# Loading first expert weights during attention, and one stage for output projection and row scaling

## The reference

```
x = x + attn_a(layernorm(x))             # 16 heads of 16, causal
    out = softmax(q k^T / 4) v           # per head
    attn_a = out @ Wo.T
n = layernorm(x);  x = x + n + moe(rmsnorm(n) * norm_scale)
    logits = t @ gate_w + gate_b; top 2 of 8 experts, softmax weights
    expert: swiglu(t @ w1 + b1) @ w2 + b2        # w1: 256 x 1024, w2: 512 x 256, each of 8 experts
x = x + attn_b(layernorm(x));  x = x + ffn(layernorm(x))
```

## Time and profile before

| | |
|---|---|
| median of 3 runs | 1952.26 us |
| the profiled execution, its own time | 1949.15 us |
| its span | 1947.3 us |
| PE busy | 1743.7 us (90%) |
| DVE busy | 1333.4 us (68%) |
| ACT busy | 826.5 us (42%) |
| POOL busy | 786.7 us (40%) |
| mean granted clock of PE | 0.93 of full speed |
| data moved by DMA | 152.83 MB, mean 78 GB/s |

### The profile page before, as it was taken

One profiled execution on the slowest core, in us unless ns is written; L12 is line 12 of the kernel. 1 busy time (PEld: TensorE's weight loads), 2 busy tenths in 40 slices (PEclk: granted clock), 3 DMA queues, 4 the chain that ended last, 5 costly groups with the idle time before them and its releaser, 6 DMA issues. The chain is left out here.

```text
span 1947.3 us, 32655 instructions
## 1 busy us (share of the span) xinstructions
PE 1743.7 (90%) x8300; PEld 977.3 (50%) x8301; DVE 1333.4 (68%) x2681; ACT 826.5 (42%) x1660; POOL 786.7 (40%) x771
## 2 busy tenths in 40 slices
PE   6979999999998667599999999699975899999997
PEld 3533443434443457356666666344444566666664
DVE  5648888878784258677776777437878577776764
ACT  3424666656666212333333333246664233333332
POOL 4341111111111004256666666243542566666663
PEclk9988999999999896599999999799995899999998
DMA  4653342424330584432222222300123222222322
GB/s 135 167 133 74 94 100 72 100 67 100 80 84 23 171 244 166 165 63 43 46 46 43 49 43 43 90 27 1 44 87 133 59 47 43 45 46 43 49 43 30
DMA packets 116124, 152.83 MB, mean 78 GB/s; under 512 B 17552, under 2 KB 98192, under 8 KB 112976
## 3 DMA queue, kind: packets, MB, share of 16 engines
q1 hardware_dynamic: 79632, 106.28, 19.7%
q0 software_dynamic: 31808, 37.32, 12.0%
q10 hardware_dynamic: 4608, 8.39, 1.2%
HBM read 86.47 MB, written 56.69 MB: 74 GB/s over the span
## 5 line engine op out<-in xcount | busy, mean ns | idle before, releaser
L502 DVE TENSOR_REDUCE a_mx<-a_p_sn 128x1 f32<-128x512 f32 (+3 forms) x640 | 371.8, 631 | 91.5 <-PE a_p_sn L541 62.9
L475 ACT ACTIVATE a_Pt<-a_p_st 128x512 f32<-128x512 f32 (+2 forms) x624 | 306.9, 577 | 194.2 <-PE a_p_st L555 179.1
L1232 ACT ACTIVATE e_y<-e_yb,wt 128x256 f32<-128x256 f32 x142 | 72.1, 508 | 502.9 <-DVE e_yb L1259 502.9
L1192 PE MATMUL e_p_y<-w,e_hT 128*128 x1136 | 271.2, 382 | 2.0 <-ACT e_hT L1226 2.0
L1171 PE MATMUL e_p_g<-w,e_tT 128*128 x568 | 270.6, 599 | 0.0
L1171 PE MATMUL e_p_l<-w,e_tT 128*128 x568 | 268.0, 594 | 0.0
L1192 PEld LDWEIGHTS e_p_y<-w,e_hT 128*128 128x128 f32 x1136 | 216.9, 191 | 92.3 <-issue 66.4
L538 PE MATMUL a_p_sn<-Kst,Qst 96*128 96x512 bf16 (+3 forms) x768 | 248.9, 344 | 8.0 <-DMA Qst<-qk_parts 5.5
L451 POOL TENSOR_SCALAR_AFFINE_SELECT a_Pt<-a_Pt 128x512 f32<-128x512 f32 x128 | 81.5, 637 | 422.3 <-ACT a_Pt L475 422.3
L555 PE MATMUL a_p_st<-Qst,Kst 99*128 99x512 bf16 (+3 forms) x768 | 215.9, 334 | 15.6 <-ACT a_Pt L475 13.1
L1080 POOL DMA_INDIRECT xs<-t_rows,token x142 | 140.3, 988 | 99.9 <-DVE token L1018 48.3
(11 more groups left out here) (208 smaller groups left out, 2532.7 us busy)
## 6 DMA issues: line engine op xcount, KB each, us to landing
qk_parts<-a_part SPq DMA_DIRECT2D x64, 192.0 KB, 2.8
a_Vst<-V SPq DMA_DIRECT2D x16, 512.0 KB, 16.3
o_rows<-a_OT ACTq DMA_DIRECT2D x32, 256.0 KB, 2.1
a_Ot<-o_rows SPq DMA_DIRECT2D x32, 256.0 KB, 3.5
...
```

What stands on the lines that cost most here:

```text
L475: act.activation(weights(kb, slice(h, h + n), a, b), p_st[:, i % RING, 0:n * (b - a)].rearrange("p (n w) -> p n w", n=n), ACT.Exp, scale=D ...
L502: dve.tensor_reduce(mx[:, hs[0]:hs[-1] + 1, place], p_sn[:, (s + k) % RING, 0:w * len(hs)].rearrange("p (h w) -> p h w", w=w), AX.X, ALU.m ...
L1192: mm = pe.matmul(p_y[:, s, 0:D], hT[:, s, k * P:(k + 1) * P], g["w2"][:, bass.ds(e, 1), k, :].rearrange("p a n -> p (a n)"), start=(k == 0 ...
```

## The change

`V` and `w1` now share one tensor `VW`: it holds 16 blocks of 4 KB per partition, which are the values of unit u during attention and one half of an expert's `w1` after it. In each SP step of `attend_a`, `load_w1(u)` writes the half u over the values of unit u, which `load_v(u)` has read by then. `project_out` and `scale_rows` become one phase `out_rows`, written out for 41 steps without a loop. In step j, tile j is turned and divided, tile j-1 turned back, tile j-2 multiplied and added with its statistics, the square roots and coefficients are made for groups of four tiles (steps 4c+5 and 4c+6), tile j-6 is normalised by ACT (it was DVE), j-7 scaled and turned, j-8 copied and made into logits. `Ot` is loaded for two tiles at a time, three slots deep, by five DMAs: four of 16 rows (the dimensions of one head, 1 KB runs) and one of the four rows of sums, so 68 rows rather than 128. The second square root is now of var(1+eps)+eps^2, and its quotient is made from both. POOL adds as soon as `n` is there. `n` and `t` lie in `R`.

```diff
+            def load_w1(u):
+                if isinstance(u, int) and u >= U - 2:
+                    sp.wait_ge(v_in, 16 * U)
+                sp.nop(nofuse=True)
+                halves = g["mlp1"].rearrange("e (k p) n -> (e k) p n", p=P)
+                sp.dma_start(g["VW"][:, bass.ds(u, 1), :].rearrange("p u n -> p (u n)"),
+                             halves[bass.ds(u, 1)].rearrange("u p n -> p (u n)")).then_inc(g["w_in"], 16)
...
+                load_w1(u)
...
-def scale_rows(nc, mem, g, t_dram, acc):
-def project_out(nc, mem, g, o_dram):
+def out_rows(nc, mem, g, o_dram, t_dram, acc):
+    C = DK + 1
+    DEEP, GROUP = 3, 4
+    Ot = mem.sb("Ot", [HG * C, DEEP, HG, 2 * P])
...
+    STEPS = NT + 9
+    def n_of(j):
+        return g["R"][:, j % 8, :]
+    def t_of(j):
+        return g["R"][:, 8 + j % 8, :]
...
+            def load(q):
+                if q >= DEEP:
+                    sp.wait_ge(rows_done, 2 * (q - DEEP) + 2)
+                b, at = 2 * q // QB, 2 * q % QB * P
+                rows = o_dram[b * HG:(b + 1) * HG, :, at:at + 2 * P].rearrange("u (h c) t -> h c u t", c=PAD)
+                for h in range(HG):
+                    sp.dma_start(Ot[DK * h:DK * (h + 1), q % DEEP], rows[h, 0:DK]).then_inc(o_in[q % DEEP], 16)
+                sp.dma_start(Ot[DK * HG:C * HG, q % DEEP], rows[:, DK]).then_inc(o_in[q % DEEP], 16)
...
+            load(0)
             sp.dma_start(wo[:, :, :], g["WoT"].rearrange("(k p) n -> p k n", p=P)).then_inc(w_in, 16)
...
+            load(1)
             sp.dma_start(srep[:, :], g["scale"].partition_broadcast(P)).then_inc(c_in, 16)
             sp.dma_start(gw[:, :, :], g["gate_w"].rearrange("(k p) e -> p k e", p=P)).then_inc(c_in, 16)
             sp.dma_start(g["gb"][:, :], g["gate_b"].partition_broadcast(P)).then_inc(c_in, 16)
...
+            for j in range(0, STEPS + 4, 2):
+                if j // 2 + 2 < NT // 2:
+                    load(j // 2 + 2)
+                if j // 2 < NT // 2:
+                    load_w2(j // 2)
...
+            def rows(j):
+                pe.wait_ge(o_in[j // 2 % DEEP], 16 * (HG + 1) * (j // 2 // DEEP + 1))
+                if j >= 2:
+                    pe.wait_ge(on_done, j - 1)
+                for u in range(HG):
+                    mm = pe.transpose(p_r[:, j % 2, u * HG * C:(u + 1) * HG * C],
+                                      Ot[:, j // 2 % DEEP, u, j % 2 * P:(j % 2 + 1) * P], g["ident"][0:HG * C, 0:HG * C])
+                mm.then_inc(rows_done, 1)
...
+            pe.wait_ge(c_in, 48)
+            for j in range(STEPS):
+                if j < NT:
+                    rows(j)
+                if 0 <= j - 1 < NT:
+                    turn_out(j - 1)
+                if 0 <= j - 2 < NT:
+                    multiply(j - 2)
+                if 0 <= j - 7 < NT:
+                    turn(j - 7)
+                if 0 <= j - 8 < NT:
+                    logits(j - 8)
...
+            def deviations(c):
+                at = slice(GROUP * c, GROUP * (c + 1))
+                act.wait_ge(mv_done, c + 1)
+                act.activation(root[:, 0, at], g["mv"][:, at, 1], ACT.Sqrt, bias=g["eps"][:, :]).then_inc(root_done, 1)
+                act.activation(root[:, 1, at], g["mv"][:, at, 1], ACT.Sqrt, bias=g["eps2"][:, :], scale=1.0 + EPS
+                               ).then_inc(root_done, 1)
+            def normal(j):
+                act.wait_ge(coef_done, 2 * (j // GROUP + 1))
+                if j >= 8:
+                    act.wait_ge(added, j - 7)
+                    act.wait_ge(t_done, j - 7)
+                act.activation(n_of(j), x_of(j), ACT.Identity, scale=inv[:, 0, j:j + 1], bias=shift[:, j:j + 1]
+                               ).then_inc(n_done, 1)
...
+            for j in range(STEPS):
+                if 0 <= j - 1 < NT:
+                    out_turned(j - 1)
+                if 0 <= j - 6 < NT:
+                    normal(j - 6)
+                if 0 <= j - 8 < NT:
+                    turned(j - 8)
+                if j % GROUP == 1 and 0 <= (j - 5) // GROUP < NT // GROUP:
+                    deviations((j - 5) // GROUP)
...
+            def coefficients(c):
+                at = slice(GROUP * c, GROUP * (c + 1))
+                dve.wait_ge(root_done, 2 * c + 2)
+                dve.reciprocal(inv[:, :, at], root[:, :, at]).then_inc(inv_done, 1)
+                dve.wait_ge(inv_done, c + 1)
+                dve.scalar_tensor_tensor(out=shift[:, at], in0=g["mv"][:, at, 0], scalar=-1.0, in1=inv[:, 0, at],
+                                         op0=ALU.mult, op1=ALU.mult).then_inc(coef_done, 1)
+                dve.tensor_tensor(inv[:, 1, at], inv[:, 1, at], root[:, 0, at], ALU.mult).then_inc(coef_done, 1)
+            def scaled(j):
+                dve.wait_ge(n_done, j + 1)
+                if j >= 8:
+                    dve.wait_ge(tp_done, j - 7)
+                    dve.wait_ge(t_out[j // GROUP % 2], 16 * (j // 8))
+                dve.scalar_tensor_tensor(out=t_of(j), in0=n_of(j), scalar=inv[:, 1, j:j + 1],
+                                         in1=srep[:, :], op0=ALU.mult, op1=ALU.mult).then_inc(t_done, 1)
+            dve.wait_ge(c_in, 48)
+            for j in range(STEPS):
+                if j < NT:
+                    inverse_sums(j)
+                if 0 <= j - 7 < NT:
+                    scaled(j - 7)
+                if j < NT:
+                    attended(j)
+                if j % GROUP == 2 and 0 <= (j - 6) // GROUP < NT // GROUP:
+                    coefficients((j - 6) // GROUP)
+                if 0 <= j - 2 < NT:
+                    add(j - 2)
+                    statistics(j - 2)
+                if j % GROUP == 1 and 0 <= (j - 5) // GROUP < NT // GROUP:
+                    moments((j - 5) // GROUP)
...
-                pool.wait_ge(t_done, j + 1)
-                x = g["X"][:, j, :]
-                pool.tensor_tensor(x, x, n[:, j % 4, :], ALU.add).then_inc(added, 1)
+                pool.wait_ge(n_done, j + 1)
+                pool.tensor_tensor(x_of(j), x_of(j), n_of(j), ALU.add).then_inc(added, 1)
...
-            pe.wait_ge(g["w_in"], 2 * 16 * NT // 2)
+            pe.wait_ge(g["w_in"], 16 * (U + NT // 2))
...
+        g["VW"] = keep.sb("values_then_w1", [P, U, QB * HG * PAD])
+        g["V"] = g["VW"][:, :, :].rearrange("p u (k h c) -> p u k h c", h=HG, c=PAD)
+        g["w1"] = g["VW"][:, :, :].rearrange("p (e k) n -> p e k n", k=KD)
...
-            g["V"] = early.sb("V", [P, U, QB, HG, PAD])
...
-        g["w1"] = keep.sb("w1", [P, E, KD, 2 * I])
...
-        phase(project_out, "a3_", o_dram)
...
-            phase(scale_rows, "s1_", t_dram, x_dram)
+            phase(out_rows, "a3_", o_dram, t_dram, x_dram)
```

More of the change, by code:

```diff
@@ L626, in tile_of @@
     return t[:, bass.ds(j, 1), :].rearrange("p a d -> p (a d)")
-def project_out(nc, mem, g, o_dram):
-    W = HG * P
-    Ot = mem.sb("Ot", [P, 2, HG, P])
+def out_rows(nc, mem, g, o_dram, t_dram, acc):
+    C = DK + 1
+    DEEP, GROUP = 3, 4
+    Ot = mem.sb("Ot", [HG * C, DEEP, HG, 2 * P])
     rec = mem.sb("rec", [P, 2, H])
@@ L772, in _ @@
                 sp.wait_ge(t_out[s], 16 * (NT // 8))
-            sp.wait_ge(x_out, 16 * (NT // 4 + 1))
-        @block.scalar
-        def _(act):
-            for r in range(2):
-                act.wait_ge(chain, 1 if r == 0 else 4)
-                act.activation(root[:, r, :], var1[:, :], ACT.Sqrt, bias=g["eps"][:, :]).then_inc(roots, 1)
-            for j in range(NT):
-                act.wait_ge(tp_done, j + 1)
-                act.copy(tT[:, j % 2, :], p_t[:, j % 2, 0:D]).then_inc(tT_done, 1)
@@ L825, in _ @@
+            sp.wait_ge(x_out, 16 * (NT // GROUP + 1))
         @block.tensor
         def _(pe):
[L827 to L837 removed]
+            def rows(j):
[6 more added lines that the diff above has]
+                mm.then_inc(rows_done, 1)
@@ L838, in _, with turn @@
+            def turn(j):
                 pe.wait_ge(t_done, j + 1)
@@ new lines, in _, with inverse_sums, attended, add @@
+        @block.vector
+        def _(dve):
+            def inverse_sums(j):
+                dve.wait_ge(rows_done, j + 1)
+                rows = p_r[:, j % 2, 0:H * C].rearrange("p (u c) -> p u c", u=HG)
+                dve.reciprocal(rec[:, j % 2, :].rearrange("p (u h) -> p u h", u=HG), rows[:, :, HG * DK:HG * C]
+                               ).then_inc(rec_done, 1)
+            def attended(j):
+                dve.wait_ge(rec_done, j + 1)
+                if j >= 2:
+                    dve.wait_ge(to_done, j - 1)
+                rows = p_r[:, j % 2, 0:H * C].rearrange("p (u c) -> p u c", u=HG)
+                dve.tensor_tensor(On[:, j % 2, :].rearrange("p (u h d) -> p u h d", u=HG, d=DK),
+                                  rows[:, :, 0:HG * DK].rearrange("p u (h d) -> p u h d", d=DK),
+                                  rec[:, j % 2, :].rearrange("p (u h) -> p u h", u=HG).unsqueeze(3).to_broadcast([P, HG, HG, DK]),
+                                  ALU.mult).then_inc(on_done, 1)
```

(15 more changed lines are left out.)

222 lines of the change are left out of this document (69 added, 153 removed).

## The result

| | before | after |
|---|---|---|
| median of the runs beside each other (lowest to highest) | 1952.24 us (1949.27 to 1952.54, 4 runs) | 1916.51 us (1914.56 to 1919.07, 4 runs) |
| the same in a later series | 1949.26 us (1945.08 to 1955.82, 14 runs) | 1919.28 us (1919.11 to 1920.67, 5 runs) |
| the profiled execution, its span | 1949.15, 1947.3 | 1919.07, 1917.3 |
| PE busy, mean granted clock | 1743.7 us, 0.93 | 1725.4 us, 0.937 |
| data moved | 152.83 MB | 148.96 MB |

The ratio is 0.9834 with a 95% interval of 0.9812 to 0.9855, in the later series 0.9844 (0.9823 to 0.9865): 30 to 36 us faster, where 28 were forecast. One execution differs from the next by more than I had assumed, so what follows compares stretches of the traces, and takes the medians only where they differ by more than 5 us.

What follows compares the result with a forecast made beforehand. The old projection was taken as bound by bytes, the scaling phase by PE at half clock; start, first eight steps 17.5, steps 8 to 31 68.0, tail 14.4 put `rank` 29.2 us earlier, less 1 for attention: 1924 us, range 1908 to 1942.

Steps and rivals of the forecast that it cites:

- first eight steps: New stage's fill: two steps at 1.2 us, three at half clock (2.9), three at 2.1; 17.5 us.
- Start: Stage's start: PE and DVE wait for `gb`, SP's 14th issue; first transposes at 658.7 us, 5.1 later than before.
- The step's chain: Plain steps of the new stage: the chain through ACT, not PE's own 2.03 us, sets the pace at 2.52 us.
- the six terms: Plain step's chain: four transposes, turn's load to ACT's copy, that copy, ACT's normalising, second copy to PE's load, logits.
- Each fourth step: Every fourth step of the stage: normalising waits for coefficients that DVE makes behind three other instructions; 3.79 us.
- The tail: From step 32 to `rank`: last product, statistics, roots, coefficients, four tiles at 0.9 us, addition and stores; 14.4 us.
- Bytes: New stage: 17 MB remain, 68 us at 250 GB/s, below the engine time, so data is no bound any more.
- Attention: Attention's loop: one `load_w1` issue per unit costs 1 us in all, between ends of 0 and 54.
- The rival that the turns pay: Attention's loop turns: five places with 3.4 us more each, 17 us more, 1941 us; chance 0.08.
- POOL and DVE: Group steps: scaling beside POOL's addition could take 0.55 us longer in each of six, 3 us more; thought rare.
- The clock: PE in the new stage: clock at 1.00 from about 665 us on, at half only in the early steps.
- The rival of half clock: PE in the new stage stays at half clock: steps of 4.04 us, 1959 us, slower than before; chance 0.07.

Runs made afterwards that it cites:

- The repeat: The changed kernel run and profiled again as it is; median 1919.28 us.
- late_constants: Changed kernel, with PE and DVE waiting for each constant only where it is used, not for all at the start; ratio 0.9844, median 1915.82 us.
- turned_first: Changed kernel, with ACT's copy of the turned `t` ahead of its two other instructions in each step; ratio 0.9794, median 1907.32 us.
- whole_rows: Changed kernel, with `Ot` read whole (128 rows, one 512 KB DMA) and turned 128 columns wide; ratio 0.9864, median 1923.88 us.
- one_later: Changed kernel, with normalising, scaling, the turn of `t` and the logits one step later (42 steps); ratio 0.9829, median 1911.43 us.
- merge_alone: Changed kernel's merged stage with narrow rows, but `V` and `w1` apart and `w1` loaded in the stage; ratio 0.9854, run again 0.9829.
- add_after_scaled: Changed kernel, with POOL's addition waiting for `t` (behind DVE's scaling) instead of for `n`; ratio 0.9831, median 1917.89 us.

## Why the prediction came out as it did

The mechanism was right in the main, and the runs show it: 1924 was forecast, 1916.5 measured. That the profiled executions came as near as 30.0 us against 28.2 is in part luck: the terms of the stage were 7.5 us too long together, and what attention and the stretch behind `rank` lost was put 5.7 us too short. Term by term, from the profiled pair:

| term | forecast | measured |
|---|---|---|
| SP's first DMA to first transposes | 9.0 | 9.3 |
| first eight steps | 17.5 | 15.0 |
| steps 8 to 31 | 68.0 (2.83 each) | 61.5 (2.56 each) |
| tail to `rank` | 14.4 | 15.6 |
| attention's end, later by | 1 | 3.7 |
| behind `rank` | 0 | 3.0 |

The repeat has 14.1, 61.5 and 16.7 in the second, third and fourth row.

- **Start.** Right, and late_constants shows that it was the wait for `gb`: 4.4 us come off the stage without it.
- **The step's chain.** Right in kind (turned_first: 1.95 us, PE's own work, which I had put at 2.03), too long by 0.17. In the plain step shown, the six terms are 0.34, 0.47, 0.27, 0.51, 0.41 and 0.36, against 0.39, 0.53, 0.28, 0.50, 0.42 and 0.40. I took the first from turns of 128 columns, where the new ones have 68, but that is 0.05 of it; the second is 0.06 and the last, my estimate from half clock, 0.04. whole_rows, with 128 columns, has 2.54 us, near the forecast's 2.52 by chance: its first term is 0.48 and its last 0.35. This is the step that failed, a size: 18 plain steps at 0.17 are 3 of the 6.5 us by which steps 8 to 31 were too long, and the six group steps are the rest.
- **Each fourth step.** Forecast 3.79, measured 3.17. 0.28 of the 0.62 stood in "0.88 by me" from transposes to the reciprocal, which is 0.60 (692.62 to 693.22), below even the 0.70 that I had as lower end from the wide turn; 0.28 in DVE's row behind it, counted too full, and the rest in ACT's copy and the logits. The coefficients' way is as described: one_later takes 0.6 of the 0.8 us off.
- **The tail.** Put at 0.9 us a tile, by ACT. Its last turns are 1.17 us apart (747.67, 748.85, 750.02), PE at half clock as in the old scaling phase, which was in my own rows; and from the last issue to `rank` it took 4.45 us, where I had 3.7.
- **Bytes.** That data is no bound came true, but my first reason (the stage loses `w1`) was idle: merge_alone has no wait for `Ot` with `w1` in the stage. My other reason, three slots of two tiles, may be it, or that the loads are spread over the whole stage rather than its first 90 us; no run has the merged stage with fewer slots. At a step of 2.0 us `w1` in the stage costs 20 us.
- **Attention.** I took 1 for 16 loads, from full work beside them, and that holds for the units between the loop's turns. The rival that the turns pay (17 us) had the right place and the wrong size: about 0.6 us more of stop at each of three turns, and with what follows the stop 3.5 us between the means. Of the 3.7 us in the table 1.3 are in attention, 2.5 ahead of it. The ranges of single traces overlap (511.9 to 516.5, and 514.4 to 521.3). I had attention ending within 2 us of 647, and called myself wrong beyond 652: the first trace has 650.3, the repeat 653.6. That attention starts later with shared V and `w1` (mean 133.2 against 131.8) I did not test; there too the ranges overlap.
- **POOL and DVE.** The group steps had none of it: scalings of 391 to 469 ns from 690 to 740 us, so the 3 us more that I had worked out did not come. In the tail it came, 945 ns in the median. It is one edit away: in turned_first each fourth scaling takes 0.85 us and its step 0.33 us longer than a plain one, in add_after_scaled the coefficients pay. On what collides the traces agree with the Trainium skill's SBUF — State Buffer, section Who interferes with whom; whether it costs depends on where the two meet.
- **The clock.** Full from 672 us rather than 665, full through the steps, half in the tail. The rival of half clock fell. But in the tail PE stood at 0.50 with 4.00 of 4.00 busy again, for 4 us, as it had for 32 us in the old scaling phase (every window from 752 to 784 us). That doesn't fit the Trainium skill's TensorE: Matmul & The Clock Gate, section What's actually happening, taken by itself, by which sustained activity releases the throttle. No run here settles why turns and logits alone don't raise it.
- **Behind `rank`.** The 3.0 us are scatter: 1158.3 to 1164.1 over all traces.
